# Repeated, unread TensorE matmuls between the stages of a four-layer kernel

## The reference

```python
x = x + _L0_conv_ref(_gn(x), ...)   # 1x1 conv, offsets, bilinear gather of 9 taps, depthwise weights
x = x + _L1_conv_ref(_gn(x), ...)   # involution: per position and channel 7x7 weights, made from x
x = x + _L2_conv_ref(_gn(x), ...)   # modulated deformable 3x3 conv: gather of 9 taps, then 128x128 weights
x = x + _L3_conv_ref(_gn(x), ...)   # attention, 8 heads of 16 channels, 2304 tokens per image
```

## Time and profile before

| | |
|---|---|
| median of 3 runs | 2131.17 us (2130.52 to 2132.05) |
| the profiled execution, its own time | 2131.18 us |
| span of its trace, first to last instruction | 2129.4 us |
| PE busy | 1685.4 us, 79% of the span |
| DVE busy | 1744.8 us, 82% |
| ACT busy | 1191.2 us, 56% |
| POOL busy | 1070.0 us, 50% |
| mean granted TensorE clock | 0.875 of full speed |

### The profile page before, as it was taken

How to read it: one execution, slowest core, us unless ns; L and a number is a source line. 1 busy time by engine, 2 the same in 40 slices (tenths; PEclk the granted TensorE clock), 3 DMA queues, 4 the chain that set the end, 5 groups by cost and what they waited for, 6 DMA issues and landing times.

```text
span 2129.4 us, 35567 instructions
## 1 busy us (share of the span) xinstructions
PE 1685.4 (79%) x11868; PEld 897.5 (42%) x11868; DVE 1744.8 (82%) x4113; ACT 1191.2 (56%) x3212; POOL 1070.0 (50%) x1229
## 2 busy tenths in 40 slices
PE   4222123149988899986999999999999999999998
PEld 2111112125554467664455555555444444444433
DVE  5888888868997799965988888888888888888871
ACT  3222223210000377654488888888777777777777
POOL 3777777735665577764877777775030000000000
PEclk8555555558999899998799999999999999999999
DMA  8677767720000466554434434432012011111101
GB/s 273 210 210 210 211 205 210 210 68 1 1 1 24 128 181 183 171 167 109 125 104 112 112 96 112 112 104 60 15 26 33 9 24 29 24 23 26 18 2 45
DMA packets 90855, 212.15 MB, mean 100 GB/s; under 512 B 18512, under 2 KB 43824, under 8 KB 90544
## 3 DMA queue, kind: packets, MB, share of 16 engines
q0 software_dynamic: 51840, 169.91, 27.1%
q1 hardware_dynamic: 38832, 39.97, 8.3%
HBM read 175.21 MB, written 13.37 MB: 89 GB/s over the span
## 4 chain that ended last, share of the span: by engine, by line
PE 45%; ACT 4%; DVE 2%; issue 2%; POOL 1%; DMA 0%; SPq 0%; ACTq 0%; POOLq 0%
PE ps L1860 14%; PE ps L1822 14%; PE ps L1838 11%; ACT l_e L1568 2%; PE ps L1918 2%; DVE l_mx L1692 1%; PE ps L1908 1%; PE ps L1845 1%; ACT corner L1539 1%; PE ps L1872 1%; POOL l_part L1435 0%; PE ps L1878 0%; POOL corner L1426 0%; PE ps L1899 0%; PE ps L1885 0%
## 5 line engine op out<-in xcount | busy, mean ns | idle before, releaser
L1692 DVE TENSOR_REDUCE l_mx<-ps 128x1 f32<-128x384 f32 x1728 | 836.1, 550 | 124.4 <-PE ps L1838 124.4
L1568 ACT ACTIVATE l_e<-ps 128x384 f32<-128x384 f32 x1728 | 727.3, 510 | 212.3 <-PE ps L1822 209.9
L1838 PE MATMUL ps<-l_ka,l_qs 96*128 96x384 bf16 x1728 | 571.6, 333 | 14.4 <-DMA l_qs<-l_part 8.8
L1822 PE MATMUL ps<-l_qs,l_ks 99*128 99x384 bf16 x1728 | 562.8, 330 | 5.2 <-ACT l_e L1568 1.8
L830 DVE SCALAR_TENSOR_TENSOR m_prod<-ps,c_b,pad 128x384 f32<-128x384 f32 x588 | 325.0, 612 | 43.7 <-PE ps L1034 42.4
L1860 PE MATMUL ps<-l_e,l_v_s 128*32 128x384 f32 x3456 | 333.4, 492 | 2.0 <-ACT l_e L1568 1.0
L552 PE MATMUL ps<-c_ident,l_samp 128*128 128x128 f32 x324 | 77.5, 423 | 312.7 <-DVE x_map L420 295.1
L1822 PEld LDWEIGHTS ps<-l_qs,l_ks 99*128 99x128 bf16 x1728 | 165.6, 97 | 360.6 <-ACT l_e L1568 193.4
L1465 POOL CAST l_nsp<-l_nm 128x3 bf16<-128x3 f32 x96 | 18.4, 191 | 522.0 <-DVE l_nm L1697 491.0
L262 POOL DMA_INDIRECT corner<-table,idx x216 | 204.8, 948 | 93.1 <-issue 65.2
L1034 PE MATMUL ps<-red,c_w 32*128 32x384 f32 x1176 | 191.9, 566 | 39.4 <-DVE m_prod L830 35.3
(11 more groups left out here) (212 smaller groups left out, 1884.4 us busy)
## 6 DMA issues: line engine op xcount, KB each, us to landing
corner<-table,idx POOLq DMA_INDIRECT x540, 3.6
l_ka<-l_part SPq DMA_DIRECT2D x96, 72.0 KB
l_ks<-l_part SPq DMA_DIRECT2D x96, 72.0 KB
table<-l_tok SPq DMA_DIRECT2D x8, 640.0 KB, 7.3
table<-red SPq DMA_DIRECT2D x8, 640.0 KB, 5.0
l_qs<-l_part SPq DMA_DIRECT2D x90, 48.0 KB
l_qs<-l_part SPq DMA_DIRECT2D x96, 24.0 KB
out<-x_map SPq DMA_DIRECT2D x12, 192.0 KB, 1.9
```

The costliest lines, as they stand in the source:

```text
L1568: nc.scalar.activation(e[:, w % 2, i, :], ps[:, st_bank(at), 0:QC], ACT.Exp).then_inc(s["st_free"], 1)
L1692: nc.vector.tensor_reduce(mx[:, ga % MAX_SLOTS, u // NQC, u % NQC:u % NQC + 1], ps[:, ab_bank(at), 0:CH], AX.X, ALU.max) \
L1822: nc.tensor.matmul(ps[:, bank, 0:QC], ks[:, head % 2, kt * 128:(kt + 1) * 128], qs[:, gb % 3, j * QC:(j + 1) * QC], start=True, stop=True) \
L1838: nc.tensor.matmul(ps[:, bank, 0:CH], qs[0:KROWS, ga // CT % 3, q0:q0 + 128], ka[:, head % 2, k0:k0 + CH], start=True, stop=True).then_inc ...
```

## The change

A helper `keep_busy` issues the same matmul a number of times, into a bank that nobody reads at that time; its result is overwritten or left. It has no semaphore of its own. In the first stage the operand is `zero` (64 x 256 zeros, called `gap` in the code), elsewhere the identity `ident` (128 x 128, fp32).

```diff
+def keep_busy(nc, bank, stationary, moving, times):
+    for _ in range(times):
+        nc.tensor.matmul(bank, stationary, moving, start=True, stop=True)
...
             @block.tensor
             def _(pe):
+                pe.wait_ge(s["gap"], 1)
+                keep_busy(nc, ps[:, 7, 0:TWIDE], gap[:, 0:128], gap, 9)
                 pe.wait_ge(g["first_loaded"], g["first_total"])
                 norm_tensor_of(nc, pe, s, t, 0)
+                keep_busy(nc, ps[:, 7, 0:TWIDE], gap[:, 0:128], gap, 5)
...
                     last.then_inc(s["out_mm"], 1)
+                    if i == ALL_TILES - 2:
+                        keep_busy(nc, ps[:, RED_BANK, 0:128], g["ident"][:, :], g["ident"][:, :], 22)
...
+                def warm(times):
+                    keep_busy(nc, ps[:, SIDE, 0:128], g["ident"][:, :], g["ident"][:, :], times)
+
+                warm(3)
                 pe.wait_ge(s["stats"], 1)
                 nc.tensor.matmul(ps[:, 0, 0:2], g["gavg"][:, :], g["mv"][:, 1, :], start=True, stop=True) \
                     .then_inc(s["means"], 1)
+                warm(10)
                 pe.wait_ge(s["norm"], 1)
...
+                warm(10)
                 pe.wait_ge(g["red_done"], CHS)
                 for step in range(STEPS):
                     q = step - LAG
+                    if step < NORM2_AT[0] and (q <= 0 or q % K7 == 0):
+                        warm(6)
                     trios = range(K7 * step // TRIO, K7 * (step + 1) // TRIO) if step < ALL_ROWS else ()
...
                 means(0, ps[:, 2, 0:2]).then_inc(s["means"], 1)
+                keep_busy(nc, ps[:, AV, 0:128], g["ident"][:, :], g["ident"][:, :], 10)
                 pe.wait_ge(s["norm"], 1)
```

## The result

The change made the kernel slower: 2142.99 us median of 5 runs (2141.82 to 2149.52) against 2131.17 us of before (2130.41 to 2133.44), a ratio of 1.0067 with a 95% interval of 1.0056 to 1.0078. That is under 1%, but the interval excludes no change. The forecast was 2128.7, with a range up to 2137. The profiled execution took 2142.89 us, 11.7 more than that of before; its span is 2141.1 us.

A forecast was written before the change was run, and what follows sets the result against it. Gathers were taken to bound the first stage and VectorE the rows. Terms of -2.5 (first stage), -3.4 (joint), -4.9 (first rows), +8.3 (ends of chunks) and 0 (attention) summed to -2.5 us: 2128.7 us, range 2121 to 2137.

The forecast's parts named there:

- The bound: Gathers pace the first stage, where only the first fetch's start counts; VectorE is the limit of the involution's rows.
- First stage: Before L496: nine repeats lift the clock, image 0's projections finish 2.5 us earlier, and the paced gathers move: -2.5 us.
- third rival: Repeats run at the low clock and delay work at L496, L1021 and L1799: 2138.8 us; chance 0.20.
- Joint: Between the first two blocks: last tile's transposes gain 0.9 us, L1021's projections 2.5, repeats hidden: -3.4 us.
- First rows: From 466.4 to 490.7 us: high clock shortens the first trio and VectorE's wait behind 24 transposes: -4.9 us.
- Ends of chunks: Steps 10 to 45, six times: six repeats delay a trio without slack; +8.3 us, clock's part taken as 0.
- Attention: Head of the attention, ten repeats before L1799: late start against faster projections, taken as 0 us.
- The second: Ends of chunks cost little or keep the clock: 2120.4 or 2122.4 us, middle 2122; chance 0.30.

## Why the prediction was wrong

Two steps failed: that the repeats of the first stage lift the clock, and that those at the ends of chunks leave the clock as it is. Between the forecast of -2.5 us and the 11.7 of the profiled pair lie 14.2 us. By the table of lags, in rounded numbers, 5.7 of them are the first stage (up to the last tile), 4.2 the ends of chunks, 2.3 the joint, 1.3 the first rows and 0.8 all behind.

**The bound** was read rightly: the stage of gathers passed its late start on (+3.0 at the first fetch, +3.2 at the last tile), and in the rows VectorE was the limit to which any lateness of PE was added.

**First stage, -2.5 (bounds -2.5 and +1.2): failed, beyond its bound.** The step was "if the nine repeats lift the clock". They didn't, and at 0.89 us they cost more than the 0.77 that I took for the low clock. Nine then ended at 9.55 instead of 8.4, behind the time at which the small matmul could start, and five started later and took 4.6 us. Measured: +3.0 at the first fetch, +3.7 us alone by the medians (+0.6 to +4.7 by the ratio's interval). The term was also too large: with 128 rows, where the clock did rise and L508 was done 2.7 to 2.8 us earlier than L496 before, the first fetch came 1.9 us earlier and the medians gained 0.2 and 0.8. That the 64 rows might not count was named, as a part of the third rival; it should have been a case with a price.

**Joint, -3.4 (bounds -3.4 and +1.5): the mechanism was right, the size off.** The first trio came 1.1 us earlier against the last tile (lag +3.2 to +2.0). I let the 22 repeats end "before 447.8" and took the clock from them; they did end, at 447.26, but the tile came at 450.95, and in these 3.68 us of idling the gained clock was lost. With 36 repeats that reach up to the tile the first trio comes 3.6 us earlier against it than before, a little more than the joint was forecast to give.

**First rows, -4.9: 3.6 measured** (lag +2.0 to -1.6). The clock was 1.00 as forecast. The wait behind the first 24 transposes went from 3.71 to 1.51 us, not to 0.46.

**Ends of chunks, +8.3: the length was right, the clock wrong.** Six waits of 1.28 to 1.41 us, 8.06 in all, as worked out from the slack of 0.04 us. But the stretch from the first 24 transposes to the sixth end grew by 12.5 us, from 179.1 to 191.5; the 4.4 us that are left go with the clock, whose part I took at 0: VectorE waits 1.65 us longer behind the transposes of the first five ends and 2.5 us longer at the sixth. The step that failed is that the repeats "stand ahead of `turn_back` and leave that stretch as long as it was". At the third end of before, PE's timeline is:

```profile
569.98 0.55 PE L1059 MATMUL ps<-c_ident,m_out_t 128*128 128x128 f32 x3
570.73 0.92 PE L1034 MATMUL ps<-red,c_w 32*128 32x384 f32 x6 [0.20 <-DVE m_prod L830]
572.31 0.92 PE L1034 MATMUL ps<-red,c_w 32*128 32x384 f32 x6 [0.65 <-DVE m_prod L830]
573.39 2.81 PE L1049 MATMUL ps<-c_ident,m_prod 128*128 128x128 f32 x24 [0.16 <-DVE x_map L845]
```

and after, as in the earlier trace rows:

```profile
569.90 1.50 PE L134 MATMUL ps<-c_ident 128*128 128x128 f32 x12
571.34 1.56 PE L1051 MATMUL ps<-red,c_w 32*128 32x384 f32 x12
572.83 0.55 PE L1076 MATMUL ps<-c_ident,m_out_t 128*128 128x128 f32 x3
574.11 0.92 PE L1051 MATMUL ps<-red,c_w 32*128 32x384 f32 x6 [0.73 <-DVE m_prod L842]
575.68 1.60 PE L1051 MATMUL ps<-red,c_w 32*128 32x384 f32 x6 [0.65 <-DVE m_prod L842]
577.21 3.79 PE L1066 MATMUL ps<-c_ident,m_prod 128*128 128x128 f32 x24
```

From the end of `turn_back` to the 24 transposes it was 2.9 us, and the clock held; it is 3.8 now, and the clock is down from 575.9 on (the trio of 1.60 us). The repeats delay the first two trios, which then go back to back, and `turn_back` with them; the trios behind it wait for VectorE, which is late by the full stall. So PE is done sooner with all that does not wait, and stands longer among the trios. At the sixth end the same time went from 2.9 to 3.9 us, and the clock fell; at the second and fifth it stayed at 2.6, and the clock held in both kernels. That the repeats bring the fall at the third end is shown: of the fourteen traces only the three with repeats ahead of the first trio have it. That they do so by the longer stretch is argued from these rows. That the place inside the stretch decides over the clock is shown by the two kernels that moved the repeats, with six at the first and fourth end in both. At the sixth end a part may be chance: in five kernels without repeats ahead of its first trio the clock fell for about 3.4 us behind that end, and in before it did not.

**Attention, 0 (bounds -0.8 and +1.5).** The ten repeats took 4.61 us at the low clock, and the projections came 1.6 us late, as at the upper bound; at the end nothing of it is left that the profiles could tell.

**The rivals.** The third, repeats that run at the low clock and make the work behind them late, happened at all three of its places, ahead of L506, L1038 and L1820, and it was given 0.20. The second, that the ends keep the clock or hide their price, was the reverse of what happened at this place, but 18 repeats in a better one gave it. The range ended at 2137 because the third rival's losses and the clock's loss at the ends, both within stated bounds, were not added up; together with the third rival's 2138.8 the 4.4 us give 2143.2. That this is the measured time is luck: the rival's price has the first stage 1.8 to 2.0 us too low, the first rows 1.3 too low and the joint 2.6 too high.

The rule that transposes do not count for the clock (the Trainium skill, TensorE: Matmul & The Clock Gate, Part 4: PE-mode transpose) was set aside on one row. A second one, of fp32 transposes as well, now speaks against it: with the repeats behind `turn_back`, 24 transposes of 5.24 us were all that PE ran from 516.08 to 521.3, and the clock, low from 514.2 on, was at 1.00 behind 521.1: the trio at 521.26 took 0.92 us again.

## What to carry to other kernels

Filler on an engine is free only in time in which that engine would wait anyway: look for the instruction behind it that still waits for someone else, as the 0.17 us of the last trio. Put it last in the gap that it is to bridge, up to the work it is meant for, since a clock gained ahead of 3.7 us of idling was gone behind them. And take as filler what the trace shows at the high clock, in the same shape: here half as many rows bought nothing for 13 us.

## What the runs showed of the hardware

- The rows of the operand decided whether repeats lifted TensorE's clock, and not its values: 13 us of dense 64-row fp32 matmuls, zeros or ones, left the matmuls behind them at 6.1 to 6.7 us, 128 rows of either brought them to 4.58.
- In the stretch of 32-row trios behind `turn_back` the clock went from 1.00 to 0.50 at four of the first six ends of chunks in the change, and at two before. With 128-row repeats ahead of the stretch's last trio, six of them (1.6 us) at the two ends where it fell before and two at three others, it stayed at 1.00 for 215 us.
